# Scan of a recurrent layer: another order of waits, inputs scaled into three pairs of PSUM banks by turns, one transfer per store

## What is computed

```python
Wx = einsum('bti,hi->bth', layernorm(t), W)            # 16 x 256 x 32
Wx = (Wx - mean) * rsqrt(var + 1e-5) * gamma + beta    # mean, var over all 4096 rows
def step(yt, wx_t):
    yt = sigmoid(wx_t + yt @ V.T)
    return yt, yt
_, ys = scan(step, zeros(16, 32), swapaxes(Wx, 0, 1))
out = t + swapaxes(ys, 0, 1)
```

## Time and profile before

| | us |
|---|---|
| median of 3 runs | 105.29 |
| the three runs | 105.41, 105.29, 101.57 |
| profiled execution | 101.73 |
| its span (first to last instruction) | 100.0 |
| TensorE busy | 82.5 |
| VectorE busy | 70.3 |
| ScalarE busy | 51.7 |
| GpSimd busy | 36.2 |
| scan, first to last product (82.55 to 94.64) | 12.09 |
| mean granted clock of TensorE | 0.996 |

### The profile page before, as it was taken

The page is one execution under the profiler, slowest core; times in us unless marked ns, Lnnn a source line. Parts: engine busy times, 40 slices in busy tenths (PEclk is TensorE's granted clock), DMA queues, the critical chain, the costliest instruction groups (busy, mean ns, idle before and its releaser), DMA issues.

```text
span 100.0 us, 2516 instructions
## 1 busy us (share of the span) xinstructions
PE 82.5 (82%) x932; PEld 58.4 (58%) x934; DVE 70.3 (70%) x194; ACT 51.7 (52%) x150; POOL 36.2 (36%) x68
## 2 busy tenths in 40 slices
PE   3999978999779899889799999899768567768840
PEld 1446654787657668578578677578534226546720
DVE  5868999849759996786793791576787568455660
ACT  5183393264172377275746835819267664555520
POOL 5710610000956937938676213029910020000030
PEclk9999999999999999999999999999999999999998
DMA  1743000000000000000000010002011000000036
GB/s 26 115 69 51 3 7 3 0 0 7 0 0 7 0 3 0 7 0 3 0 7 0 0 52 7 0 0 59 0 52 52 0 0 0 0 3 0 0 82 135
DMA packets 8460, 1.87 MB, mean 19 GB/s; under 512 B 7392, under 2 KB 8448, under 8 KB 8448
## 3 DMA queue, kind: packets, MB, share of 16 engines
q1 hardware_dynamic: 7920, 1.58, 8.0%
q10 hardware_dynamic: 528, 0.13, 0.6%
HBM read 0.66 MB, written 0.52 MB: 12 GB/s over the span
## 4 chain that ended last, share of the span: by engine, by line
PE 58%; DVE 23%; ACT 9%; issue 7%; DVEq 0%
PE pair L1307 8%; PE pair L1626 7%; PE pair L1419 6%; PE pair L1146 5%; PE pair L1382 4%; DVE z L896 3%; ACT warm L768 3%; PE pair L1335 3%; DVE max_b L868 2%; DVE max_b L870 2%; PE pair L1273 2%; PE pair L1389 2%; DVE xnT L811 2%; PE pair L1359 2%; PE pair L1354 2%
## 5 line engine op out<-in xcount | busy, mean ns | idle before, releaser
L1626 PE MATMUL pair<-warm,w_bd 128*128 128x124 f32 (+3 forms) x44 | 7.6, 295 | 3.3 <-ACT warm L768 2.0
L576 ACT ACTIVATE eqk<-pair 128x512 f32<-128x512 f32 x16 | 8.8, 604 | 2.7 <-PE pair L1257 2.7
L446 POOL TENSOR_TENSOR z<-z 128x512 f32<-128x512 f32 x4 | 5.1, 1265 | 13.6 <-DVE z L896 13.6
L1307 PE MATMUL pair<-ctxo,eqk 64*128 64x66 f32 x128 | 8.9, 277 | 1.0 <-DVE z L896 0.8
L1307 PEld LDWEIGHTS pair<-ctxo,eqk 64*128 64x128 f32 x128 | 7.9, 187 | 2.1 <-issue 1.7
L1626 PEld LDWEIGHTS pair<-warm,w_bd 128*128 128x128 f32 x44 | 5.8, 188 | 5.4 <-DVE pair L1096 4.0
L1096 DVE COPY pair<-wxn 128x248 f32<-128x248 f32 (+3 forms) x13 | 5.5, 422 | 4.5 <-ACT warm L768 3.7
L613 ACT ACTIVATE eqk<-pair 128x384 f32<-128x384 f32 x16 | 7.2, 498 | 2.6 <-PE pair L1401 2.5
L1146 PE MATMUL pair<-idle_b 128*128 128x512 bf16 x19 | 6.9, 489 | 1.5 <-DVE idle_b L789 1.5
L768 ACT ACTIVATE warm<-pair 128x124 f32<-128x124 f32 (+2 forms) x20 | 5.0, 275 | 4.5 <-PE pair L1626 4.5
L935 DVE TENSOR_REDUCE smax_b<-pair 128x2 bf16<-128x256 f32 x8 | 3.4, 425 | 4.1 <-PE pair L1359 4.0
(11 more groups left out here) (189 smaller groups left out, 206.9 us busy)
## 6 DMA issues: line engine op xcount, KB each, us to landing
x_tok<-in_x_dram SPq DMA_DIRECT2D x8, 64.0 KB, 2.5
eqk<-t SPq DMA_DIRECT2D x8, 64.0 KB, 2.1
out_dram<-out_tok SPq DMA_DIRECT2D x3, 128.0 KB, 2.6
out_dram<-out_tok ACTq DMA_DIRECT2D x1, 128.0 KB, 2.7
w_raw<-in_L_conv_w_qkv_dram SPq DMA_DIRECT2D x1, 48.0 KB, 2.4
wout_sb<-in_L_conv_w_out_dram SPq DMA_DIRECT2D x1, 16.0 KB, 2.3
brow<-in_L_conv_b_out_dram SPq DMA_DIRECT2D x1, 16.0 KB, 2.9
gln_bc<-in_L_conv_g_ln_dram SPq DMA_DIRECT2D x1, 16.0 KB, 2.6
```

The source lines that it names most:

```text
L576: act.activation(eqk[:, r, g], bank[g][:], ACT.Exp).then_inc(s_expA, 1)
L1307: ins = pe.matmul(opair[:, f, n * (2 * h + a):n * (2 * h + a + 1)], eqk[at, r, 2 * i + a, h * P:(h + 1) * P], ctxo[at, r % 2, 2 * i + a, : ...
L1626: pe.matmul(part(c, s)[:, :, j0:], vT_bd, src, start=False, stop=True, skip_group_check=True).then_inc(s_pre[c], 1)
```

## The change

- The two waits of a product are written the other way round, and only chain 0 waits for the seed.
- `input_of`, the array `wxn` and `seed_1` are gone from the scan. `seed(s)` scales `wxT` straight into PSUM, all 256 elements at every step. Three pairs of banks take turns, so a seed waits for the sigmoids of step s-3. All 14 seeds stand ahead of the output adds.
- Chains are now rounds (0, 1) and (2, 3), and images are dealt to rounds differently, so that one transfer can cover all 128 partitions: the first two stores become one of 256 KB, the last two are split by image groups.
- Two fillers go to bank 5, the one on bank 4 is the last, there is one fewer, and one waits for the last copy of `wxT`. The small product of the statistics goes to bank 7.

```diff
-        vote_bank = bank[2 * ((STEPS + 1) % 2)]
+        parts = [(pair[0], pair[1], mid_pair)[s % 3] for s in range(STEPS)]
+        vote_bank = parts[STEPS - 1][:, 0]
 
         def part(c, s):
 
-            return bank[2 * (s % 2) + c][:, 0:RPC * CHUNKS].rearrange("p (r j) -> p r j", r=RPC)
+            return parts[s][:, c, 0:RPC * CHUNKS].rearrange("p (r j) -> p r j", r=RPC)[:, :, 0:CHUNKS - place(s)[2]]
 
         def turned(m):
 
-            return (opair, mid_pair, opair, pair[STEPS % 2])[m][:, :, 0:P]
+            return (opair, parts[WARM + 1], opair, parts[WARM + 2])[m][:, :, 0:P]
...
-        by_chunk = out.rearrange("(f b) q (j m) k -> f (q j) b m k", f=RPC, m=STRIDE)
-
-        def store(engine, f, ms, n):
+        by_chunk = out.rearrange("(g c f) q (j m) k -> g (f q j) c m k", g=G, c=CHAINS, m=STRIDE)
+
+        def store(engine, gs, ms, n):
 
             engine.wait_ge(s_fin, n)
-            engine.dma_start(by_chunk[f, :, :, ms].rearrange("j b m k -> j b (m k)"),
-                             out_tok[f * CHUNKS:(f + 1) * CHUNKS, :, :, ms].rearrange("j c g m k -> j (c g) (m k)"))\
-                .then_inc(s_stored, 16)
+            engine.dma_start(by_chunk[gs, :, :, ms].rearrange("g p c m k -> p (g c) (m k)"),
+                             out_tok[:, gs, :, ms].rearrange("p g c m k -> p (g c) (m k)")).then_inc(s_stored, 16)
...
-                                 x.rearrange("b (h q) w c -> h (q w) b c", h=HALVES)[h, :, G * r:G * (r + 1)])\
+                                 x.rearrange("(g r) (h q) w c -> h r (q w) g c", h=HALVES, r=R)[h, r])\
...
-            store(sp, 0, slice(0, 2), 2)
-            store(sp, 1, slice(0, 2), 2)
-            store(sp, 0, slice(2, STRIDE), 5)
+            store(sp, slice(0, G), slice(0, 2), 2)
+            store(sp, slice(0, G // 2), slice(2, STRIDE), 5)
...
-            store(act, 1, slice(2, STRIDE), 5)
+            store(act, slice(G // 2, G), slice(2, STRIDE), 5)
...
             def seed(s):
-                m, at, j0 = place(s)
-                if s <= STRIDE + 1:
-                    dve.wait_ge(s_wxn, min(s - 1, STRIDE))
-                if s >= 3:
+                if s >= 4:
                     for c in range(CHAINS):
-                        dve.wait_ge(s_y[c], s - 1)
-                dve.tensor_copy(pair[s % 2][:, :, 0:RPC * CHUNKS].rearrange("p c (r j) -> p c r j", r=RPC)[:, :, :, j0:],
-                                wxn[:, m].rearrange("p (r c) j -> p c r j", c=CHAINS)[:, :, :, j0 + at:CHUNKS + at])\
-                    .then_inc(s_seed, 1)
+                        dve.wait_ge(s_y[c], s - 2)
+                dve.tensor_scalar(parts[s][:, :, 0:RPC * CHUNKS].rearrange("p c (r h j) -> p c r h j", r=RPC, h=HALVES),
+                                  wxT[:].rearrange("p (c r) (h m j) -> p m c r h j", c=CHAINS, h=HALVES, m=STRIDE)
+                                  [:, place(s)[0]], bn_sc[:, 4:5], bn_sc[:, 6:7], ALU.mult, ALU.add).then_inc(s_seed, 1)
 
             dve.wait_ge(s_full, 1)
-            seed_1()
-            for s in range(2, STRIDE + 2):
-                input_of(place(s)[0])
+            for s in range(1, STEPS):
+                if s == STRIDE + 2:
+                    dve.memset(state[:, :, STRIDE - 1:], 0.0).then_inc(s_state, 1)
                 seed(s)
-            dve.memset(state[:, :, STRIDE - 1:], 0.0).then_inc(s_state, 1)
-            for s in range(STRIDE + 2, STEPS - 1):
-                seed(s)
...
             residual(0, both, 1).then_inc(s_fin, 1)
-            seed(STEPS - 1)
             residual(1, both, 2).then_inc(s_fin, 1)
...
             awake(3)
-            awake(0)
-            awake(1)
-            awake(2)
-            pe.matmul(bank[3][:], idle_b[:, 0:P], idle_b[:], start=True, stop=True).then_inc(s_full, 1)
+            awake(5)
+            pe.wait_ge(s_wxS, R)
+            awake(5)
+            pe.matmul(bank[4][:], idle_b[:, 0:P], idle_b[:], start=True, stop=True).then_inc(s_full, 1)
...
-                    pe.wait_ge(s_seed, s)
                     pe.wait_ge(s_y[c], s)
-                    pe.matmul(part(c, s)[:, :, j0:], vT_bd, src, start=False, stop=True,
+                    if c == 0:
+                        pe.wait_ge(s_seed, s)
+                    pe.matmul(part(c, s), vT_bd, src, start=False, stop=True,
                               skip_group_check=True).then_inc(s_pre[c], 1)
```

More of the change, by code:

```diff
@@ L47, in conv_attn_rnn @@
     RPC = R // CHAINS
+    STORES = 3
     FIRST = 0.5
@@ L173, in conv_attn_rnn @@
         resid = eqk[:, 0, 0:CHAINS, :].rearrange("p n (m g c) -> p n m g c", m=STRIDE, g=G)
-        out_tok = sb("out_tok", [P, CHAINS, G, STRIDE, C])
+        out_tok = sb("out_tok", [P, G, CHAINS, STRIDE, C])
         diff = eqk[:, 1, 0, 0:R * (CHUNKS - 1)].rearrange("p (r j) -> p r j", r=R)
@@ L364, in residual_out @@
                 for h in range(HALVES):
-                    at = (r // CHAINS) * CHUNKS + h * (CHUNKS // 2)
-                    sp.dma_start(resid[at:at + CHUNKS // 2, r % CHAINS].rearrange("j m g c -> j m (g c)"),
-                                 t2[:, r, h * G:(h + 1) * G].rearrange("p g c -> p (g c)")).then_inc(s_res[r % CHAINS], 16)
+                    at = (r % RPC) * CHUNKS + h * (CHUNKS // 2)
+                    sp.dma_start(resid[at:at + CHUNKS // 2, r // RPC].rearrange("j m g c -> j m (g c)"),
+                                 t2[:, r, h * G:(h + 1) * G].rearrange("p g c -> p (g c)")).then_inc(s_res[r // RPC], 16)
             residual_out(0)
@@ L372, in _ @@
             residual_out(3)
-            store(sp, 0, slice(0, 2), 2)
-            store(sp, 1, slice(0, 2), 2)
-            store(sp, 0, slice(2, STRIDE), 5)
+            store(sp, slice(0, G), slice(0, 2), 2)
+            store(sp, slice(0, G // 2), slice(2, STRIDE), 5)
             with step_by_step(sp):
[L377 to L380, removed]
+                store(sp, slice(0, G), slice(0, STRIDE), 9)
+                sp.wait_ge(s_stored, 16 * (STORES + 1))
+            sp.wait_ge(s_stored, 16 * STORES)
         @block.gpsimd
@@ L766, in _ @@
                         act.wait_ge(s_pre[c], s)
-                        src = part(c, s)[:, :, j0:]
+                        src = part(c, s)
                     act.activation(dst, src, ACT.Sigmoid).then_inc(s_y[c], 1)
-            store(act, 1, slice(2, STRIDE), 5)
+            store(act, slice(G // 2, G), slice(2, STRIDE), 5)
             with step_by_step(act):
@@ L1057, in _ @@
             dve.wait_ge(s_bnp, 1)
-            dve.tensor_scalar(bn_sc[:, 2:3], bank[5][:, 0:1], -1.0, None, ALU.mult)
-            link(dve.tensor_scalar(bn_sc[:, 3:4], bank[5][:, 1:2], EPS, None, ALU.add))
-            dve.scalar_tensor_tensor(out=bn_sc[:, 0:1], in0=bank[5][:, 0:1], scalar=bn_sc[:, 2:3],
+            dve.tensor_scalar(bn_sc[:, 2:3], bank[7][:, 0:1], -1.0, None, ALU.mult)
+            link(dve.tensor_scalar(bn_sc[:, 3:4], bank[7][:, 1:2], EPS, None, ALU.add))
+            dve.scalar_tensor_tensor(out=bn_sc[:, 0:1], in0=bank[7][:, 0:1], scalar=bn_sc[:, 2:3],
                                      in1=bn_sc[:, 3:4], op0=ALU.mult, op1=ALU.add).then_inc(s_bnve, 1)
@@ L1069, in _ @@
             dve.wait_ge(s_wxS, R)
[L1071 to L1087, removed]
@@ L1111, in residual @@
                 dve.wait_ge(s_yT, ready)
-                return dve.tensor_tensor(out_tok[:, c, :, m], turned(m)[:, c].rearrange("p c (g k) -> p c g k", g=G),
+                return dve.tensor_tensor(out_tok[:, :, c, m].rearrange("p g c k -> p c g k"), turned(m)[:, c].rearrange("p c (g k) -> p c g k", g=G),
                                          resid[:, c, m], ALU.add)
@@ L1131, in _ @@
             with step_by_step(dve):
-                dve.wait_ge(s_stored, 16 * R)
+                for m in range(STRIDE):
+                    ins = dve.tensor_scalar(wxn[:, m].rearrange("p r (h j) -> p r h j", h=HALVES),
+                                            wxT[:].rearrange("p r (h m j) -> p m r h j", h=HALVES, m=STRIDE)[:, m],
+                                            bn_sc[:, 4:5], bn_sc[:, 6:7], ALU.mult, ALU.add)
+                ins.then_inc(s_wxn, 1)
+                dve.wait_ge(s_stored, 16 * STORES)
                 for m in range(STRIDE):
@@ L1603, in _ @@
             pe.wait_ge(s_bnin, 1)
-            pe.matmul(bank[5][:, 0:2], groupavg[:].rearrange("p g c -> p (g c)"), bn_mv[:],
+            pe.matmul(bank[7][:, 0:2], groupavg[:].rearrange("p g c -> p (g c)"), bn_mv[:],
                       start=True, stop=True).then_inc(s_bnp, 1)
@@ L1639, in _ @@
             with step_by_step(pe):
+                pe.wait_ge(s_wxn, 1)
                 with pe.Fori(0, CHUNKS) as j:
                     for m in range(STRIDE):
-                        pe.matmul(bank[m % 4][:, 0:R].rearrange("p (c r o) -> p c r o", c=CHAINS, o=1), ident[:],
-                                  wxn[:, m].rearrange("p (r c) j -> p c r j", c=CHAINS)[:, :, :, bass.ds(j, 1)],
-                                  start=True, stop=False)
```

(1 more changed line is left out.)

2 lines of the change are left out of this document (1 added, 1 removed).

## The result

| us | before | after |
|---|---|---|
| runs | 105.41, 105.29, 101.57, 101.84 | 99.95, 99.88, 100.11, 99.95 |
| median | 103.56 | 99.95 |
| profiled execution | 101.73 | 99.95 |
| its span | 100.0 | 98.2 |
| first product, its weights | 82.55 | 82.23 |

The kernels compare as 0.983, with a 95% interval of 0.981 to 0.985: 1.7 us less, short of the 2% that can be told from no change. Forecast were 100.5 us (99.8 to 104.3; the likeliest case alone 99.9 to 101.0) and -1.2%. Executions of one kernel fall into groups that differ by TensorE's mean granted clock, and every comparison here is of the lowest group (mean clock 0.96 or more), unless a sentence names another.

A forecast was written before the change was run, and what follows sets the result against it. A latency ring of product, sigmoid and issue, with no engine full, was taken to bound the scan. Thirteenth step 1.12 earlier (0.24+12 x 0.06+0.16), fourteenth 1.25, so the end 1.2: 101.73-1.2 = 100.5 us, range 99.8 to 104.3.

The forecast's parts named there:

- the likeliest case: Whole kernel: all terms come as priced, 100.5 us, own range 99.9 to 101.0; chance 0.50.
- Link: Sigmoid to next product in the scan: exchanging the two waits gains 0.06 a step, 0.91 to 0.85, 0.78 over 13 links.
- Start of the scan: Last coefficient to first product: one filler fewer and one 0.55 scaling for two instructions; product at 82.31 not 82.55, gain 0.24.
- VectorE through the scan: Seeds on VectorE: ready 0.7 to 0.8 us early, hiding the stalled step (0.16) and the late last seed (0.07).
- the pause: VectorE's 0.41 stall at 87.28 with nothing to wait for: cost 0.16 before, to cost nothing with the lead.
- Stores: Tail: data bound it, so the end moves only with the earlier stores, 1.2; double transfer 0 to 0.7 late.
- Loads and residual copies, statistic product: Loads in other batches, same number and sizes: 0, at most 0.3 either way; statistic product to another free bank: 0.
- 1: Scan: the exchange of waits does nothing, steps stay 0.91, only 0.47 gained, 101.3 us; chance 0.12.
- 2: Tail: the double store's data is late, 0.65 given back, 101.2 us; chance 0.05.
- 4: Scan: weights load while the sigmoid still runs, 0.16 a link, 2.1 plus 0.47, 99.2 us; chance 0.05.
- 3: Scan: TensorE falls to 1.2 GHz, 0.20 more a step, 3.3 in all, 103.8 us; chance 0.28 with the upper group.
- the ring: Scan: repeating waits of product 0.47, sigmoid 0.28 and issue 0.14, turning in 0.91 us with no engine full.

The follow-up runs named there:

- two pairs: The kernel after with two pairs of PSUM banks by turns instead of three, a seed waiting for the sigmoids of two steps before: 0.989, 100.45 to 100.59 us.
- stores alone: The kernel before with only the changed stores, dealing of images and loads, its waits and seed stages as they were: 0.996, 0.45 us less.
- stores undone: The kernel after with four stores of 64 partitions and 128 KB each, as before: 0.990, 100.49 to 100.92 us.

## Why the prediction was right, and where not

- **Link.** Right to the hundredth: sigmoid to weights 0.05, step 0.85. Undoing it in the kernel after costs 0.80, where 0.78 was forecast. Alone it brings half of that.
- **Start of the scan.** Right: 0.24. The first product came at 82.23 and not 82.31 because all ahead of it was 0.08 sooner. The new scaling took 546 ns for the 0.55 taken. The Trainium skill's rule that an fp32 operation with an operand in PSUM has the plain rate (VectorE: DVE Perf Modes, Why PSUM operands drop a tier) agrees with the rows: 546 into PSUM here, 406 within SBUF.
- **VectorE through the scan.** Right: no wait of TensorE for a seed after the first, the pause costs no step, and the last step is 0.85. A seed was ready 0.86 before its product (85.91+0.55 = 86.46 for 87.32), where 0.7 to 0.8 was forecast. Together 0.78+0.16+0.07 = 1.01 was forecast and 1.03 came. The two pairs show that the lead was needed at every second step; my "even at 0.83 each it fits the step nearly" was not tried and is doubtful.
- **Stores.** This is the step that failed. That the time still lies in the likeliest case's own range (from 99.9) is luck: its lower bound stood for 0.10 a link, which did not come. I wrote that "the data bound the tail" and priced the shape at nothing, or up to 0.7 late. The end moved with the first store, as said (1.20, where 1.12 and 1.25 stood), but behind it 0.57 more were gained, of which the runs ascribe 0.45 to 0.6 to the 128 partitions (stores alone 0.45, stores undone 0.6). The share of 0.87 at 181 GB/s in the earlier trace rows was read as full; it was an average over a stretch at 200 GB/s and one at half of that, and it left out the 1.3 us between issue and first data. The term should have been -0.5, and the sum 100.0.
- **Loads and residual copies, statistic product.** 0 was priced, and that is right like for like: a later run of the kernel after with a mean clock of 1.00 has the coefficient at 81.39 (before 81.40) and its first product at 82.30. The 0.08 go with TensorE's clock early in the kernel. In the trace after, the two transposes at 5.40 and at 7.82 us take 0.44; in the trace before, those at 5.82 and 8.12 take 0.69. Of both kernels the runs with a mean clock near 0.98 lie 0.1 below those near 1.00 (before 101.45 to 101.66 and 101.72 to 101.86; after 99.86 to 99.97 and 100.02 to 100.11).
- **Rivals.** 1: fell, by the 0.04 of issue and by undoing the order. 2: fell; the double issue takes 0.41, less than one of 64 partitions. 4: fell. The Trainium skill's rule that TensorE pulls weight loads ahead (TensorE: Matmul & The Clock Gate, Step-by-step: what each phase is for) speaks of matmuls that run. It did not reach to this rival, whose matmul waits: in every step after the first the first load starts 0.05 behind the sigmoid. 3: TensorE's clock does fall in the scan in some executions, but none of the four of the kernel after is that slow. The price was 0.31 a step and not 0.20: I had added the longer pass to the ring, but four passes with their loads at 1.2 GHz take 1.19, so the ring is gone and TensorE is the bound. The 421 ns of the earlier trace rows were read rightly, since the transposes in the stretch at 0.50 take 391 in the median and 421 at most, which speaks against the 9 in the clock row; the 328 beside it is the longest one in the scan, where the median is 273. That the 3.3 in all came near the 3.6 of the runs is luck: the step was priced too low, and the drop came only at the fourth product. It was no answer to this change: the group at 105 of the kernel before is in all likelihood the same thing (the trace is of the kernel with the stores alone), which "what separates the groups no row shows" left open.

## To carry to other kernels

Where a product has two waits, let it carry the one that comes last. Look at who is really late, for the bracket named the carried one here. It pays in full only if the other wait is over early: exchange and lead together brought what neither did alone. And read a tail in slices of 0.1 us before calling it bound by data: a mean of 0.87 hid a dip between transfers, and the gap from issue to first data lay outside its stretch.

## What was not expected of the hardware

- A store of 64 partitions is issued in 0.64 us on SP's queue and 0.75 on ScalarE's; one of 128 partitions with the same bytes in 0.41 and 0.47; with twice the bytes still in 0.41. Its first data comes 0.9 us behind the start of the issue instead of 1.3.
- A separate wait instruction in front of a product costs 0.06 us: the weights come 0.11 behind the end of what it waits for, and 0.05 where the product carries the wait.
- VectorE pauses once in the scan for some 0.4 us with nothing to wait for, at 87.28 before and near 88.5 after. Its cause is not known; the trace with two pairs does not have it. Here a lead of a step hid it.
- At 1.2 GHz a step is 1.22 instead of 0.91, a third more, with TensorE busy for 0.97 of it.
